# Twice the identity folded into the scaled linear weights of both layers, in place of a matmul (first layer) and a VectorE addition (second layer) of twice x

## The reference, cut to what matters

```python
def layer(x):                                  # both layers, with their own weights
    agg = segment_sum(messages(x[dst], edge_attr), src)
    u0, u1 = bilinear(x, agg)                  # 64 scalars, 32 vectors
    ud0 = x0 @ lu0 / sqrt(64)                  # the linear map, scalars
    ud1 = einsum('euk,uv->evk', x1, lu1) / sqrt(32)   # vectors
    return x + merge(u0 + ud0, u1 + ud1)
x = layernorm(x + layer_0(x))
x = layernorm(x + layer_1(x))
```

## Time and profile before

| | us |
|---|---|
| time, median of 3 runs | 7061.11 (7058.83 to 7061.15) |
| span of the profiled execution | 7384.0 |
| first stage | up to some 2500 |
| first layer's tiles (sum_edges of tile 0 to that of tile 99) | 2515 to 5349 |
| second layer's tiles (sum_edges of tile 0 to the end) | 5539 to 7384 |

### The profile page before, as it was taken

How to read it: one execution, slowest core, us unless ns; L and a number is a source line. 1 busy time by engine, 2 the same in 40 slices (tenths; PEclk the granted TensorE clock), 3 DMA queues, 4 the chain that set the end, 5 groups by cost and what they waited for, 6 DMA issues and landing times.

```text
span 7384.0 us, 145782 instructions
## 1 busy us (share of the span) xinstructions
PE 5898.2 (80%) x52295; PEld 4739.6 (64%) x52295; DVE 5535.0 (75%) x7299; ACT 3742.5 (51%) x11578; POOL 5548.6 (75%) x4491
## 2 busy tenths in 40 slices
PE   5666666666666588888898989988849999999999
PEld 3444444545544477777776777777737777777777
DVE  5666666767666577777777777777728999998888
ACT  2232322323232355555555555555527777777776
POOL 3787877788878567777777777777757888888887
PEclk6777777777777799999999999999969999999999
DMA  7877777777776366776776777677632222222222
GB/s 219 244 229 223 230 218 224 224 225 232 224 221 194 107 203 229 234 234 222 232 242 223 239 237 228 227 236 231 211 118 93 94 94 94 94 94 95 95 96 75
DMA packets 681151, 1381.01 MB, mean 187 GB/s; under 512 B 106047, under 2 KB 487661, under 8 KB 654447
## 3 DMA queue, kind: packets, MB, share of 16 engines
q1 hardware_dynamic: 527695, 1090.23, 46.7%
q0 software_dynamic: 152736, 281.45, 11.3%
HBM read 587.20 MB, written 784.08 MB: 186 GB/s over the span
## 4 chain that ended last, share of the span: by engine, by line
PE 50%; DVE 13%; issue 12%; ACT 11%; another core or an unknown queue 8%; POOL 3%; SPq 1%; DMA 1%; DVEq 0%; POOLq 0%; ACTq 0%
PE node_ps L1373 13%; PE prods_ps L1341 5%; PE prods_ps L1322 5%; ACT onehot L1722 4%; PE prods_ps L1325 3%; DVE zs L1054 3%; PE node_ps L1390 3%; PE m_ps L1238 2%; PE s_ps L1238 2%; PE m_ps L1390 2%; POOL slots L649 2%; PE turn_ps L1360 2%; PE s_ps L1220 2%; PE node_ps L1238 2%
## 5 line engine op out<-in xcount | busy, mean ns | idle before, releaser
L649 POOL DMA_INDIRECT slots<-pay,slot_all x3136 | 3282.2, 1047 | 905.8 <-issue 835.5
L1722 ACT ACTIVATE onehot<-node_iota,msgs 128x125 f32<-128x125 f32 x3400 | 1030.2, 397 | 75.4 <-POOLq L711 75.4
L1373 PEld LDWEIGHTS node_ps<-msgs,onehot 128*125 128x125 f32 x6800 | 931.9, 188 | 149.3 <-issue 108.8
L1373 PE MATMUL node_ps<-msgs,onehot 128*125 128x160 f32 x6800 | 980.6, 303 | 45.8 <-ACT onehot L1728 32.7
L1104 DVE TENSOR_REDUCE upd<-work 125x48 f32<-125x3072 f32 x300 | 1003.9, 3346 | 6.9
L1091 DVE TENSOR_TENSOR work<-prods_ps,yv 125x1024 f32<-125x1024 f32 x800 | 930.9, 1216 | 35.6 <-PE prods_ps L1326 24.5
L1220 PE MATMUL s_ps<-ident,picks_sb 128*125 128x128 f32 x1568 | 377.2, 383 | 574.8 <-issue 486.3
L751 POOL TENSOR_TENSOR q<-xt,yv 125x3072 f32<-125x3072 f32 x100 | 547.7, 5477 | 339.6 <-PE turn_ps L1360 323.0
L1238 PE MATMUL m_ps<-win,picks_sb 125*128 125x160 f32 x3136 | 673.5, 343 | 104.7 <-issue 62.5
L724 POOL TENSOR_TENSOR q<-xt,yv 125x512 f32<-125x512 f32 x400 | 428.3, 1073 | 383.9 <-PE turn_ps L1360 360.7
L1220 PEld LDWEIGHTS s_ps<-ident,picks_sb 128*125 128x125 f32 x1568 | 306.4, 271 | 621.3 <-issue 610.2
(11 more groups left out here) (274 smaller groups left out, 14481.9 us busy)
## 6 DMA issues: line engine op xcount, KB each, us to landing
msgs<-slots SPq DMA_DIRECT2D x200, 1428.0 KB, 6.4
slots<-zero SPq DMA_DIRECT2D x183, 1386.0 KB
win<-table SPq DMA_DIRECT2D x784, 160.0 KB
picks<-picks_sb SPq DMA_DIRECT2D x196, 512.0 KB
picks_sb<-picks SPq DMA_DIRECT2D x196, 512.0 KB
table<-tab SPq DMA_DIRECT2D x200, 350.0 KB
slots<-pay,slot_all POOLq DMA_INDIRECT x3136
spill_in<-spill_sums SPq DMA_DIRECT2D x200, 80.0 KB, 6.0
```

The lines of the kernel that those rows point to most:

```text
L649: g.indirect_dma_start(out=slots[layer][:, :], out_offset=bass.IndirectOffsetOnAxis(ap=slot_all[:, j:j + 1], axis=0), in_=pay[q][:, j - UB ...
L1373: te.matmul(node_ps[0:HM, 0:D], onehot[:, j, :], msgs[b][:, j, 0:D], start=(j == 0), stop=False)
L1722: last = ac.activation(onehot[:, j, :], node_iota[:, :], ACT.Square, bias=msgs[b][:, j, LOCAL:LOCAL + 1], scale=-1.0)
```

## The change

Twice the identity is added to the linear weights when they are scaled, so that 2x comes out of the linear map itself. The matmul L1386 of the first layer is gone, and L1387 and L1388 now start their own columns of the bank in both layers. In the second layer the VectorE instruction L1135 and its wait are gone. The two scalings (L889 for `lin0`, and L891) become a multiply and add with a view of `ident2`. The semaphore `lin_out` of the second layer is no longer made.

```diff
-            for n in (("picked", "weighed", "pick_turned", "pick_out"), ("copied", "mixed_mul"))[layer]:
+            for n in (("picked", "weighed", "pick_turned", "pick_out", "lin_out"), ("copied", "mixed_mul"))[layer]:
...
-                            (t.vv[:, :, :], "u_vv"), (t.lin0[0:S, :], "l_s"))
+                            (t.vv[:, :, :], "u_vv"))
...
                     if part == 1:
-                        last = ve.tensor_scalar(t.lin_u[:, :].rearrange("p (u i) -> p i u", i=3), t.lin1[:, :].rearrange("p (i u) -> p i u", i=3),
-                                                float(k["l_v"]), None, ALU.mult)
+                        ve.scalar_tensor_tensor(t.lin0[0:S, :], t.lin0[0:S, :], float(k["l_s"]), ident2[0:S, 0:S], ALU.mult, ALU.add)
+                        last = ve.scalar_tensor_tensor(t.lin_u[:, :].rearrange("p (u i) -> p i u", i=3), t.lin1[:, :].rearrange("p (i u) -> p i u", i=3),
+                                                       float(k["l_v"]), ident2[0:3 * V, 0:3 * V].rearrange("p (i u) -> p i u", i=3), ALU.mult, ALU.add)
...
                     ve.wait_ge(s["upd"], R1 * n + R1)
-                    if layer == 1:
-                        ve.scalar_tensor_tensor(m_ps[0:HM, 0:D], xt[nb][0:HM, :], 2.0, m_ps[0:HM, 0:D], ALU.mult, ALU.add).then_inc(s["lin_out"], 1)
-                        ve.wait_ge(s["lin_out"], n + 1)
                     ve.tensor_tensor(h[0:HM, :], lin[0:HM, :] if layer == 0 else m_ps[0:HM, 0:D], upd[0:HM, :], ALU.add).then_inc(s["h_ready"], 1)
...
                     to = (node_ps, m_ps)[layer]
-                    if layer == 0:
-                        te.matmul(to[0:HM, 0:D], ident2[0:HM, 0:HM], xt[nb][0:HM, :], start=True, stop=False)
-                    te.matmul(to[0:HM, S:D], v_t[nb][:, :], w.lin_u[:, :], start=layer == 1, stop=layer == 1)
-                    te.matmul(to[0:HM, 0:S], x2_t[nb][:, :], w.lin0[:, :], start=layer == 1, stop=False)
+                    te.matmul(to[0:HM, S:D], v_t[nb][:, :], w.lin_u[:, :], start=True, stop=True)
+                    te.matmul(to[0:HM, 0:S], x2_t[nb][:, :], w.lin0[:, :], start=True, stop=False)
```

More of the change, by code:

```diff
@@ L290, in layer_sems @@
             for n in ("hot", "edges_done", "y_out", "y_turned", "y_turned_out", "prods", "prods_used", "upd", "q_mul", "q_part", "ss_out",
-                      "q_turned", "q_turned_out", "lin", "lin_out", "h_ready", "deviation", "inverse", "normed",
+                      "q_turned", "q_turned_out", "lin", "h_ready", "deviation", "inverse", "normed",
                       "msg", "pay_out", "located",
```

## The result

The change makes the kernel slower: 7133.05 us (median of 4 runs, 7132.9 to 7135.27) against 7059.97 for the kernel before, a ratio of 1.0104 [1.009, 1.0119]. I had forecast 7045.7 us, in a range that ended at 7066.

The account below looks back on a forecast made before the run. The prediction took PE and what it waits for to set the pace, with GpSimd nearly level in the first layer. It summed 13.0 + 2.0 + 0.4 = 15.4 us of gain to 7045.7 us, range 7028 to 7066.

Parts of the forecast that it names:

- The second layer: Second layer: removing VectorE's addition gains nothing, hidden behind PE's round 0, except 0.4 us behind the last tile.
- The matmul's 0.28 us: First layer, PE: without L1386 all that follows `linear` comes 0.28 us earlier, 28 us for 100 tiles.
- The slack: First layer: GpSimd has 3.19 us of slack a step in the profile, perhaps less in the timed runs.
- the middle, 0.14 us a step: First layer, 93 steps with scatters: half of the 0.28 us gained on each, 13.0 us in all.
- the rival with a chance of 0.25: GpSimd paces the first layer in timed runs; only the first seven steps and the end gain, 2.4 us, 7059; chance 0.25.
- the bound: First layer: a saving on one of two level engines is worth between 0 and 0.28 us a step.
- The first seven steps: First layer, where GpSimd scatters nothing yet: the whole 0.28 us gained on each, 2.0 us.
- The clock: First layer: PE waits early at `turn_q` more often and falls to half clock, 5.0 us a step; 7083; chance 0.09.
- What I said would show it: Signs, first layer: PE busy about 25.8 us a step, GpSimd's L724 wait smaller; second: 18.30 us steps, 0.65 us before `zs`.

Follow-up runs that it names:

- `e11_before_q2`: The kernel before the change, with VectorE's product of the first component one place later in VectorE's order; 7027.72 us, 0.9958 of the kernel before.
- `e6_qfirst_2`: The changed kernel, with VectorE's product of the first component one place later in VectorE's order; 7021.43 us, 0.9948 of the kernel before.

## Why the prediction was wrong, point by point

*The second layer* was right. It keeps 18.30 us a tile, the addition is gone, and the idle time ahead of `zs` is 0.66 us, for which I had 0.65:

```profile
6009.14 0.33 DVE L1135 TENSOR_TENSOR h<-m_ps,upd 125x160 f32<-125x160 f32 x1
6010.11 2.31 DVE L1055 TENSOR_TENSOR zs<-prods_ps,spill_tab 128x1000 f32<-128x1000 f32 x2 [0.66 <-PE prods_ps L1321]
```

*The matmul's 0.28 us* on PE were right as well: 25.74 to 25.46 us a step where PE paces (`e11_before_q2`, `e6_qfirst_2`), and 0.30 us from L1383 to L1384, the first two of `linear`, for which I had 0.29.

```profile
3349.22 0.46 PE L1383 MATMUL node_ps<-w_lin_u,spill_tab 96*125 96x96 f32 x2 [0.66 <-ACT q_t L1618]
3349.52 0.35 PE L1384 MATMUL node_ps<-w_lin,spill_tab 128*125 128x64 f32 x2
```

*The slack* was read from the profile with the pauses. I took GpSimd's 26.03 us to lie near PE's and chose the middle, 0.14 us a step gained. In the timed runs GpSimd paces at 26.08 against PE's 25.74, so the rival with a chance of 0.25 was right about who paces. The 26.03 itself was close. PE's 26.8 was not: the mean clock of 0.97 in the earlier trace rows comes from 14 stretches at the half clock, and undisturbed PE needs 25.74 with its wait. PE and GpSimd stood the other way round than I read them.

*The step that failed* is the bound: "between none and all of it, on each step". I treated GpSimd's step as a number of its own that PE can at best leave as it is. It is not: 1.80 of its 26.08 us are lost beside VectorE's operations, and which are met depends on when PE releases VectorE. The lower end of the bound had to go below nought, to -0.97 us a step; 92 of these would be 89 us. After the change 51 of the 92 steps are at 27.0 to 27.1 us and the others hold or follow a fall of the clock, but for the first five, with 2467.0 us in all against 2396.1, and 70.9 us of loss. The first seven steps, counted at 2.0 us of gain, lost 1.4: five gained 0.27 to 0.28 us each, and a fall of the clock in another cost 3.0. The trace could have told me of the bound: its mean of 1075 ns for the issues mixes 0.96 with values up to 2.0, and the prediction takes the mean, without the spread or what ran beside the long ones.

*The clock*, my rival for a slower kernel, saw something that happens but not the cause of the loss. Falls come with the shorter step: 9 after, none before, from tile 7 on. Where PE paces (`e6_qfirst_2`) each lasts 3.4 us and costs 27.02 - 25.46 = 1.56 us, behind no wait but the 0.66 us. In the changed kernel five last 3.4 us, in steps of 28.61 us, and four 10.2 us, in steps of 31.2, which is 4.2 us over 27.05 and near the 5.0 that I read from the earlier trace rows. Busy times by window, one of the four and the 26.6 us ahead of it (columns as in the earlier trace rows):

```profile
3728.20:3754.80 26.60, 24.19 (x241) 19.62 (x240) 21.64 (x18) 16.00 (x55) 22.22 (x20) 1.00 0.78 252
3754.80:3765.00 10.20, 10.02 (x54) 8.94 (x54) 6.53 (x5) 5.00 (x18) 8.37 (x9) 0.50 0.74 259
```

PE waits there for VectorE's second addition ahead of `turn_q` by some 1.5 us, in steps with a fall and in most others of 27.05 (67 waits above). The falls are not what makes the kernel slow: each puts the phase right for a few steps, with one to four of 25.46 us behind it, and 28.61 + 25.46 + 25.94 = 80.0 us are less than three steps of 27.05.

*What I said would show it:* GpSimd's wait at L724 did get smaller, but to nothing, and not through the change. "PE busy for about 25.8 us a step" was a number of the disturbed profile.

## What to carry to other kernels

Where an engine paces that shares something with another, its step is no constant. Before costing a saving elsewhere at "nothing or better", look at the spread of its instructions' durations and at what runs beside the long ones, and ask what the saving moves in time against them. The loss was cheap to mend here: one line moved in VectorE's order gave 112 us back (7133 to 7021), and relieving GpSimd of one half product 122. That adding work made a kernel faster, 0.41 us on VectorE here, was the sign that the phase is the cause and not the amount of work.

## What the runs showed of the hardware

An indirect DMA issue on GpSimd of 0.96 us ends only 0.83 to 0.95 us behind a VectorE operation with two SBUF inputs that began ahead of it by as little as 0.09 us (1.95 us in all). It is not touched by one that begins 0.16 us behind it, nor by a sum of the same length with one SBUF input, nor by a multiplication of the same length with one input in PSUM. GpSimd's half product, two SBUF inputs of its own, took 1.30 to 1.39 us in place of 1.08 when it began 0.75 to 0.83 us into the same operation; when it began 0.13 to 0.46 us into it, VectorE's operation was the one held up, to 2.3 to 2.6 us.
